# An LSTM kernel: the adds of high and low rows split by gates between VectorE and GpSimd, and VectorE's order around them

## The reference

```python
xW = jnp.einsum('ntd,dg->ntg', x, Wx) + b      # x (16, 512, 512), Wx (512, 2048)
def step(carry, xw_t):
    prev_h, prev_c = carry
    a = xw_t + prev_h @ Wh                      # Wh (512, 2048)
    i = jax.nn.sigmoid(a[:, :Hdim])
    f = jax.nn.sigmoid(a[:, Hdim:2 * Hdim])
    o = jax.nn.sigmoid(a[:, 2 * Hdim:3 * Hdim])
    g = jnp.tanh(a[:, 3 * Hdim:])
    next_c = f * prev_c + i * g
    next_h = o * jnp.tanh(next_c)
    return ((next_h, next_c), next_h)
_, hs = jax.lax.scan(step, (h0, zeros), swapaxes(xW, 0, 1))
return x + swapaxes(hs, 0, 1)
```

## Time and profile before

| what | value |
|---|---|
| median of 3 runs | 1969.94 us (1966.04 to 1971.7) |
| the profiled execution | 1969.25 us, of which its span is 1967.5 us |
| PE busy | 1895.6 us, 96% of the span |
| PEld busy | 1682.2 us, 86% |
| DVE busy | 1708.7 us, 87% |
| ACT busy | 1021.3 us, 52% |
| POOL busy | 237.9 us, 12% |
| granted TensorE clock | 0.999 of full |

### The profile page before, as it was taken

One profiled execution on the slowest core, in us unless ns is written; L12 is line 12 of the kernel. 1 busy time (PEld: TensorE's weight loads), 2 busy tenths in 40 slices (PEclk: granted clock), 3 DMA queues, 4 the chain that ended last, 5 costly groups with the idle time before them and its releaser, 6 DMA issues.

```text
span 1967.5 us, 145698 instructions
## 1 busy us (share of the span) xinstructions
PE 1895.6 (96%) x65588; PEld 1682.2 (86%) x65588; DVE 1708.7 (87%) x8715; ACT 1021.3 (52%) x4241; POOL 237.9 (12%) x526
## 2 busy tenths in 40 slices
PE   1999999999999999999999999999999999999998
PEld 0888888888888888888888888888888888888887
DVE  8888888888888888888888888888888888888887
ACT  4455555555555555555555545555555555555554
POOL 0111111111111111111111111111111111111111
PEclk9999999999999999999999999999999999999999
DMA  5000000000000000000000000000000000000000
GB/s 198 15 26 21 21 26 21 21 23 24 21 21 26 21 21 26 21 21 23 23 21 21 26 21 21 26 22 21 21 26 21 21 25 21 21 21 26 18 13 15
DMA packets 39216, 51.56 MB, mean 26 GB/s; under 512 B 4416, under 2 KB 36160, under 8 KB 38592
## 3 DMA queue, kind: packets, MB, share of 16 engines
q1 hardware_dynamic: 37152, 37.77, 6.0%
q10 hardware_dynamic: 1440, 4.49, 0.6%
HBM read 25.46 MB, written 16.78 MB: 21 GB/s over the span
## 4 chain that ended last, share of the span: by engine, by line
PE 95%; DVE 2%; issue 1%; DMA 1%; ACTq 0%; ACT 0%; DVEq 0%
PE acc L265 45%; PE acc L271 27%; PE acc L277 23%; DMA wh<-in_wh 1%; DVE wx_low L345 0%; DVE wh_low L345 0%; DVE turned L443 0%; PE x_sums L318 0%; DVE products L451 0%; DVE wh_low L343 0%; DVE preact L447 0%; DVE gates L461 0%; DVE w_tops L331 0%; DVE wx_low L343 0%; DVE o_gate L456 0%
## 5 line engine op out<-in xcount | busy, mean ns | idle before, releaser
L265 PE MATMUL acc<-wx_high,x_halves 128*32 128x256 f16 x16384 | 937.2, 273 | 5.2 <-ACT acc L208 2.6
L265 PE MATMUL acc<-wx_low,x_halves 128*32 128x256 f16 x16384 | 935.5, 273 | 0.5 <-issue 0.3
L271 PE MATMUL acc<-wh_low,h_halves 128*32 128x256 f16 x16384 | 722.9, 274 | 21.9 <-DVE wh_low L345 4.0
L277 PE MATMUL acc<-wh_high,h_halves 128*32 128x256 f16 x16384 | 719.4, 273 | 0.7 <-issue 0.4
L222 ACT ACTIVATE gates<-preact 128x96 f32<-128x96 f32 x1024 | 290.4, 284 | 800.6 <-POOL preact L168 773.3
L443 DVE STREAM_TRANSPOSE turned<-acc 128x256 f32<-128x256 f32 x1024 | 460.8, 450 | 192.8 <-PE acc L277 183.0
L271 PEld LDWEIGHTS acc<-wh_low,h_halves 128*32 128x32 f16 x16384 | 384.0, 96 | 165.1 <-DVE h_halves L468 138.8
L265 PEld LDWEIGHTS acc<-wx_high,x_halves 128*32 128x32 f16 x16384 | 465.3, 97 | 26.7 <-ACT acc L208 9.6
L265 PEld LDWEIGHTS acc<-wx_low,x_halves 128*32 128x32 f16 x16384 | 465.1, 97 | 11.2 <-issue 3.9
L277 PEld LDWEIGHTS acc<-wh_high,h_halves 128*32 128x32 f16 x16384 | 423.3, 96 | 31.6 <-issue 2.8
L168 POOL TENSOR_TENSOR preact<-turned 128x128 f32<-128x128 f32 x512 | 235.3, 460 | 1724.5 <-DVE turned L443 1724.5
(11 more groups left out here) (61 smaller groups left out, 295.2 us busy)
## 6 DMA issues: line engine op xcount, KB each, us to landing
out<-out_ring SPq DMA_DIRECT2D x128, 128.0 KB, 1.7
x_ring<-in_x SPq DMA_DIRECT2D x120, 128.0 KB, 2.3
wx<-in_wx ACTq DMA_DIRECT2D x4, 512.0 KB, 8.1
wx<-in_wx SPq DMA_DIRECT2D x4, 512.0 KB, 8.1
wh<-in_wh SPq DMA_DIRECT2D x4, 512.0 KB, 16.7
wh<-in_wh ACTq DMA_DIRECT2D x4, 512.0 KB, 17.2
x_ring<-in_x SPq DMA_DIRECT2D x2, 512.0 KB, 16.5
b_rows<-in_b ACTq DMA_DIRECT2D x1, 256.0 KB, 21.3
```

The lines of the kernel that those rows point to most:

```text
L265: pe.matmul(acc[par][n][32 * j:32 * j + 32, 0:GL], x_halves[:, slot, c], w[:, c, n * Q + j], start=False, stop=False, skip_group_check=True)
L271: pe.matmul(acc[par][n][32 * j:32 * j + 32, 0:GL], h_halves[1 - par][:, c, 0:2], w_low["wh"][:, c, n * Q + j], start=False, stop=False, sk ...
L277: last = pe.matmul(acc[par][n][32 * j:32 * j + 32, 0:GL], h_halves[1 - par][:, c, 1:3], w_high["wh"][:, c, n * Q + j], start=False, stop=c ...
```

## The change

`preact` of group 0 was added by POOL in one instruction of 128 elements a partition and that of group 1 by DVE likewise. Now DVE adds the three cell gates (96 elements) of both groups with `add_three`, POOL adds the output gate (32 elements) of group 0, and DVE that of group 1 with `add_last`. ACT's `last_gate` gets a wait of its own, for `o_preact_ready`. On DVE, `add_three(0)` goes between the transposes, `add_three(1)` behind `gate_products(0)`, `add_last(1)` ahead of `gate_products(1)`, `high_of_h(0)` ahead of `new_cell(1)`, and `high_of_h(1)` ahead of `full_h(1)`. `high_of_h` waits for both factors with one semaphore that output gate and cell tanh both increment, and `full_h` no longer waits. On PE the wait for `x_ready` ahead of the input matmuls is made once in a chunk and not once in a quarter. `low_of_h(1)` waits for `h_feat_ready` and not for `h_high_ready`.

The diff, without the declarations of semaphores:

```diff
@@ -165,7 +165,8 @@
 
             for t in range(T):
                 pool.wait_ge(turned_ready, NG * t + 1)
-                pool.tensor_tensor(preact[0][:], turned[0][:, :, 0, :], turned[0][:, :, 1, :], ALU.add).then_inc(preact_ready[0], 1)
+                pool.tensor_tensor(preact[0][:, 6:8], turned[0][:, 6:8, 0, :], turned[0][:, 6:8, 1, :], ALU.add)\
+                    .then_inc(o_preact_ready[0], 1)
 
         @block.scalar
         def _(act):
...
@@ -218,18 +219,19 @@
                 if t + 1 < T:
                     place_bias(t + 1)
                 def three_gates(n):
-                    act.wait_ge(preact_ready[n], t + 1)
+                    act.wait_ge(preact_ready, NG * t + n + 1)
                     act.activation(gates[par][n][:, 1:4, :], preact[n][:, 0:6].rearrange("p (g c) b -> p g (c b)", c=2), ACT.Tanh,
                                    scale=rescale[chunk % 2]).then_inc(gates_ready, 1)
 
                 def last_gate(n):
+                    act.wait_ge(o_preact_ready[n], t + 1)
                     act.activation(gates[par][n][:, 4, :], preact[n][:, 6:8].rearrange("p c b -> p (c b)"), ACT.Tanh,
                                    scale=rescale[chunk % 2]).then_inc(o_ready, 1)
 
                 def tanh_of_cell(n):
                     act.wait_ge(cell_ready, NG * t + n + 1)
                     act.activation(cell_tanh[n][:], gates[1 - par][n][:, 0, :], ACT.Tanh, scale=0.5)\
-                        .then_inc(cell_tanh_ready, 1)
+                        .then_inc(h_parts_ready[n], 1)
 
                 three_gates(0)
                 last_gate(0)
...
@@ -308,7 +310,7 @@
                 recurrent_low(par, 1, (2, 3))
                 recurrent_high(par, 1, (2, 3)).then_inc(acc_ready, 1)
                 if t + 1 < T:
-                    if (t + 1) % QUARTER == 0:
+                    if at + 1 == CHUNK:
                         pe.wait_ge(x_ready, (t + 1) // QUARTER + 1)
                     for n in range(NG):
                         pe.wait_ge(bias_placed, NG * (t + 1) + n + 1)
...
@@ -442,9 +444,14 @@
                     dve.wait_ge(acc_ready, nth[n])
                     dve.transpose(turned[n][:].rearrange("p g s b -> p (g s b)"), acc[par][n][:, 0:GL]).then_inc(turned_ready, 1)
 
-                def add_halves(n):
+                def add_three(n):
                     dve.wait_ge(turned_ready, nth[n])
-                    dve.tensor_tensor(preact[n][:], turned[n][:, :, 0, :], turned[n][:, :, 1, :], ALU.add).then_inc(preact_ready[n], 1)
+                    dve.tensor_tensor(preact[n][:, 0:6], turned[n][:, 0:6, 0, :], turned[n][:, 0:6, 1, :], ALU.add)\
+                        .then_inc(preact_ready, 1)
+
+                def add_last(n):
+                    dve.tensor_tensor(preact[n][:, 6:8], turned[n][:, 6:8, 0, :], turned[n][:, 6:8, 1, :], ALU.add)\
+                        .then_inc(o_preact_ready[n], 1)
 
                 def gate_products(n):
                     dve.wait_ge(gates_ready, nth[n])
...
@@ -454,7 +461,7 @@
                 def output_gate(n):
                     dve.wait_ge(o_ready, nth[n])
                     dve.tensor_scalar(o_gate[n][:], gates[par][n][:, 4, :], 1.0, scales[following][:, 1:2], ALU.add, ALU.mult)\
-                        .then_inc(o_gate_ready, 1)
+                        .then_inc(h_parts_ready[n], 1)
 
                 def new_cell(n):
                     dve.wait_ge(products_ready, nth[n])
...
@@ -463,40 +470,35 @@
 
                 def high_of_h(n):
                     og, ct = (k[n][:].rearrange("p (c b) -> p c b", b=B) for k in (o_gate, cell_tanh))
-                    if n == 0:
-                        dve.wait_ge(cell_tanh_ready, nth[0])
+                    dve.wait_ge(h_parts_ready[n], 2 * (t + 1))
                     dve.tensor_tensor(h_halves[par][:, 2 * n:2 * n + 2, 1, :], og, ct, ALU.mult).then_inc(h_high_ready, 1)
 
                 def full_h(n):
                     og, ct = (k[n][:].rearrange("p (c b) -> p c b", b=B) for k in (o_gate, cell_tanh))
-                    if n == 1:
-                        dve.wait_ge(o_gate_ready, nth[1])
-                        dve.wait_ge(cell_tanh_ready, nth[1])
                     dve.tensor_tensor(h_feat[par][:, 2 * n:2 * n + 2, :], og, ct, ALU.mult).then_inc(h_feat_ready, 1)
 
                 def low_of_h(n):
                     cs = slice(2 * n, 2 * n + 2)
-                    if n == 0:
-                        dve.wait_ge(h_feat_ready, nth[0])
-                    else:
-                        dve.wait_ge(h_high_ready, NG * (t + 1) + 2)
+                    dve.wait_ge(h_feat_ready, nth[n])
                     dve.tensor_tensor(h_halves[par][:, cs, 2, :], h_feat[par][:, cs, :], h_halves[par][:, cs, 1, :], ALU.subtract)\
                         .then_inc(h_ready, 1)
 
                 turn(0)
+                add_three(0)
                 turn(1)
-                add_halves(1)
                 gate_products(0)
+                add_three(1)
                 output_gate(0)
                 new_cell(0)
+                add_last(1)
                 gate_products(1)
+                high_of_h(0)
                 new_cell(1)
-                high_of_h(0)
                 full_h(0)
                 output_gate(1)
                 low_of_h(0)
+                high_of_h(1)
                 full_h(1)
-                high_of_h(1)
                 low_of_h(1)
 
                 half, slot = divmod(at, HALF)
```

6 lines of the change are left out of this document (3 added, 3 removed).

## The result

The changed kernel takes 1937.41 us (median of 4, 1933.95 to 1940.52), the kernel before in the same comparison 1967.99 us (median of 4). The ratio is 0.9847, with a 95% interval of 0.9825 to 0.9868: 1.5% faster. The forecast was 1952 us in a range of 1926 to 1980. The profiled execution took 1937.38 us, its span is 1935.5 us, 32 us less than before.

The account below looks back on a forecast made before the run. A chain of small operations that leaves a hole in PE was taken as the bound. 1969.25 - 20 (0.04 a step, 512 steps) + 3 (bias waits) = 1952 us; range 1926 to 1980, the forecast's own 1944 to 1962.

Parts of the forecast that it names:

- What bounds: Whole step: a chain of small operations closes a hole in PE of about 0.2 us a step.
- fast rival: PE does not feel the low halves of h: step 3.61 us, 1924 us in all; chance 0.11.
- parts 1 and 2: Group 0's three gates added on VectorE: ScalarE starts at 0.78, products(0) at 1.10 us after turn(0); gain 0.24.
- part 3: add_three(1) ahead of output_gate(0) and new_cell(0): new_cell(0) at 1.55 instead of 1.62 us, 0.07 of gain left.
- part 4: GpSimd's add of 32 elements is hidden; add_last(1) sits in VectorE's wait for ScalarE and costs nothing.
- rival of a collision: GpSimd and VectorE reads collide, products(0) held until 1.21: step 3.79 us, 2010 us in all; chance 0.13.
- part 5: high_of_h(0) ahead of new_cell(1) ends at 2.23 instead of 2.33 us; PE can load it 0.10 earlier.
- parts 6 and 7: Low halves come no earlier; PE stalls 0.03 and 0.04 us on them; step 3.68 instead of 3.71, gain taken 0.04.
- steps with a bias wait: Input matmuls wait for a bias once a chunk, over a smaller hole: 0.1 us for 31 chunks, 3 us charged.
- low_of_x: In 4 of 16 steps it may hold turn(0) for 0 to 0.07 us, at most 9 us; taken as nothing.

Follow-up runs that it names:

- e10: Changed kernel without the 32 input matmuls a step that use wx_low; 1929.75 us, ratio 0.9707 to the kernel before.
- e7: Changed kernel with GpSimd's add of 32 elements waiting for the vector engine's first add; 1958.35 us, one run.
- e11: Changed kernel with one more GpSimd add of 128 elements a step, result unused, after the vector engine's first add; 1977.92 us, one run.
- e2: Changed kernel with an unused vector multiply of 32 elements between high_of_h(0) and new_cell(1); 1985.35 us, ratio 1.0036 to the kernel before.

## Why the prediction was right, and where its sizes were off

**What bounds.** Right. The time alone would not say so: 1937 us lies under the 1944 to 1962 that the forecast gave as its own range, and is nearly as close to the fast rival's 1924 as to 1952. It is the rows and the experiments that decide. The hole in PE was closed by a chain of small operations, and e10 shows that a quarter of PE's matmuls can go without the step changing.

**The first gates earlier (parts 1 and 2).** Right to the hundredth: add_three(0) took 0.26 (between the bounds of 0.29 and 0.18), ScalarE started 0.78 behind turn(0), products(0) 1.09 where 1.10 was forecast.

**The inserted add (part 3).** Right: new_cell(0) at 1.55.

**GpSimd and add_last hidden (part 4).** Right, and the rival of a collision was real in kind: both orders of holding exist (e7, e11). It had no price here, since GpSimd comes second and is done long before products(0).

**The high half (part 5) and the low halves (parts 6 and 7).** The mechanism was right: the loop changes its closing point from the high half of group 0, which e2 rules out for the changed kernel, to the low half of group 1, as its trace shows, and each low half is now waited for. With it the fast rival, in which only the high half counts, is refuted: its step was 3.61. The size was off. Forecast was a step of 3.68 and a gain of 0.04; measured 3.65 and 0.071. The terms that were mis-sized are small, and all but one are of one sign. The hand-over from ScalarE to VectorE was taken as 0.04; the new trace has 0.03 at each of the three places that lie on this path (1002.83 to 1002.86, 1003.77 to 1003.80, and before high_of_h(1)). low_of_h(1) follows full_h(1) after 0.03, too, and ended 3.14 behind turn(0) and not 3.17. The load went 0.05 and not 0.06 behind the low half, and the 0.01 between a load and its matmul isn't there. Against these 0.05 stands 0.02, since turn(0) comes 0.46 and not 0.44 behind a matmul that had to wait. That makes 3.65 of 3.68. A sum of fifteen terms read at 0.01 can't be better than this, and all the gain hung on its last 0.04; the range had allowed for 0.02 to 0.06, which was too narrow.

**The steps with a bias wait.** Charged with 3 us. In the changed kernel on chip 1, turn(0) to turn(0) in the step with the bias wait (place 14 of a chunk):

```profile
1045.58 0.45 DVE L445 STREAM_TRANSPOSE turned<-acc 128x256 f32<-128x256 f32 x1 [0.23 <-PE acc L279]
...
1049.36 0.45 DVE L445 STREAM_TRANSPOSE turned<-acc 128x256 f32<-128x256 f32 x1
```

and in the one behind x_sums (place 8):

```profile
1023.64 0.45 DVE L445 STREAM_TRANSPOSE turned<-acc 128x256 f32<-128x256 f32 x1 [0.24 <-PE acc L279]
...
1027.35 0.45 DVE L445 STREAM_TRANSPOSE turned<-acc 128x256 f32<-128x256 f32 x1 [0.38 <-PE acc L279]
```

3.78 and 3.71 where 3.65 is typical: 0.13 and 0.06 more, for 31 chunks 6 us. In the kernel before the same two places have 3.72, as all others (medians). The bias was rightly seen; that x_sums' matmul also needs the hole was missed, 2 us.

**low_of_x.** Taken as nothing, rightly: it runs until 0.08 behind the start of turn(0), which isn't held (it starts at 1005.02 and lasts until 1005.50, turn(0) starts at 1005.42 and the step is 3.65).

**What was not in the prediction.** PE's standing still at the boundaries of its instruction blocks, 9.4 us before and 15.7 us after on chip 1, up to 83.7 us elsewhere. A hole in PE was read as lost time only. It is also what swallows such stalls, and a change that narrows it lays them bare. On chip 1 the forecast mechanism gave 1.5%; on chip 3 the same kernel gave 0.7%.

## What to carry to other kernels

When one rendezvous closes a loop, list the others with their room before pricing a gain: here the next one stood 0.07 us behind, and moving work on the same queue spends its room. Undoing each half of a change showed that neither half is worth anything alone, so a change in an ordered queue has to be tried with the order that lets it through. A hole in the bounding engine is not free time to be removed: measure what it hides, and compare kernels on one chip, since what it hides differed between chips by more than the last improvement.

## What the runs showed of the hardware that was not expected

- PE stands still inside a row of equal matmuls, without a semaphore, for up to 0.6 us (1112.95 to 1113.56). In the waits its input loads do so 23 to 209 times in an execution with 128 matmuls a step, never with 96, and more often on some chips than on others. All 1585 such places in thirteen traces lie at one number out of every 256 of PE's instructions, which come in packets of 16 KB, and end 1.18 to 1.62 us behind the landing of a packet.
- GpSimd's add of 128 x 32 elements takes 0.25 us alone and 0.32 beside a vector add with two SBUF operands; with 128 elements it is 0.46 and 0.53. A vector instruction with two SBUF operands that becomes ready 0.19 to 0.20 us ahead of the end of GpSimd's add is held for 0.05 us, one that becomes ready 0.09 to 0.14 ahead of it is not held.
